# A gated Mamba block with a mixture of experts on one Trainium2 core: another table of items for the four scan batches

## What is computed

```
x  = silu(conv4(in_proj @ ctx) + conv_b)             # 512 channels x 512 steps, a causal convolution of 4 taps
dt_low, B, C = split(x_proj @ x)                     # 16 + 16 + 16 rows
dt = softplus(dt_proj @ dt_low + dt_proj_b)
for each state n of 16, each channel d of 512:
    h[n,d,t] = exp(dt[d,t] * A[d,n]) * h[n,d,t-1] + dt[d,t]*x[d,t]*B[n,t]
y[d,t] = sum over n of h[n,d,t] * C[n,t]  + D[d]*x[d,t]
x_tok += tanh(g) * y * silu(layernorm(x_tok))        # z is the layernorm of the tokens
```

## Time and profile before

| | us |
|---|---|
| median of 3 runs | 1016.52 (1015.74 to 1017.32) |
| the profiled execution's own time | 1012.7 |
| span of its trace | 1010.9 |
| scans of batches 0, 1, 2, 3 | 122.9, 109.3, 102.8, 95.5 |
| from the first scan to the end of the last | 430.5 |

### The profile page before, as it was taken

The page is one execution under the profiler, slowest core; times in us unless marked ns, Lnnn a source line. Parts: engine busy times, 40 slices in busy tenths (PEclk is TensorE's granted clock), DMA queues, the critical chain, the costliest instruction groups (busy, mean ns, idle before and its releaser), DMA issues.

```text
span 1010.9 us, 20635 instructions
## 1 busy us (share of the span) xinstructions
PE 891.2 (88%) x5397; PEld 752.7 (74%) x5397; DVE 738.8 (73%) x1112; ACT 593.1 (59%) x1006; POOL 571.0 (56%) x504
## 2 busy tenths in 40 slices
PE   6898789887988878877999999899999999974796
PEld 3465677566756767766999999899999898863795
DVE  5888989999999999999676676444554554555376
ACT  3669989797989999893332133334544444543121
POOL 5246996888968998987011057232534534531363
PEclk9799979999999999999999999999999999995699
DMA  8106111420115114113111157654657766664476
GB/s 278 44 21 229 33 42 43 154 89 31 53 38 205 42 48 135 44 49 120 42 42 42 53 174 297 213 191 168 232 182 237 238 184 237 227 199 132 139 246 225
DMA packets 65870, 136.39 MB, mean 135 GB/s; under 512 B 8833, under 2 KB 13441, under 8 KB 65666
## 3 DMA queue, kind: packets, MB, share of 16 engines
q1 hardware_dynamic: 54528, 104.68, 31.9%
q0 software_dynamic: 8960, 29.37, 8.1%
q10 hardware_dynamic: 2306, 1.33, 0.6%
HBM read 162.48 MB, written 42.07 MB: 202 GB/s over the span
## 4 chain that ended last, share of the span: by engine, by line
PE 33%; SPq 5%; POOL 5%; issue 5%; ACT 2%; DVE 2%; ACTq 1%; DMA 1%; POOLq 0%; DVEq 0%
PE psY L993 10%; PE psG L957 9%; PE psU L957 9%; POOL slot_in L641 3%; PE psT L950 2%; PE psHT L971 2%; POOL weights L666 1%; SPq L469 1%; SPq L525 1%; SPq L524 1%; ACT weights L1258 1%; SPq L526 1%; SPq L463 1%; SPq L509 1%; DMA xin<-xn_rows 1%
## 5 line engine op out<-in xcount | busy, mean ns | idle before, releaser
L597 POOL TENSOR_TENSOR prod<-hst,cbc 128x512 f32<-128x512 f32 x256 | 327.4, 1312 | 76.6 <-PE y_ps L804 39.5
L1507 DVE TENSOR_TENSOR_SCAN hst<-dA,dbu_ps 128x512 f32<-128x512 f32 x256 | 298.8, 1202 | 20.1 <-issue 10.1
L782 PE MATMUL dbu_ps<-ident,dbuT 128*128 128x128 f32 x1008 | 165.6, 288 | 45.9 <-DVE hst L1507 37.0
L782 PEld LDWEIGHTS dbu_ps<-ident,dbuT 128*128 128x128 f32 x1008 | 115.0, 145 | 107.8 <-DVE hst L1507 68.3
L1305 ACT CAST hh<-psHT 128x384 fp32r<-128x384 f32 x79 | 37.8, 478 | 252.8 <-PE psHT L971 252.8
L1179 ACT ACTIVATE dbuT<-duT,BT 128x512 f32<-128x512 f32 x252 | 160.7, 709 | 17.5 <-PE dbu_ps L782 15.6
L1169 ACT ACTIVATE dA<-dts,Aneg 128x512 f32<-128x512 f32 x256 | 166.4, 709 | 0.2
L804 PE MATMUL y_ps<-ident,prod 128*128 128x128 f32 x1024 | 159.1, 281 | 6.0 <-POOL prod L597 5.3
L957 PE MATMUL psU<-weights,xh 128*128 (+2 forms) x560 | 142.8, 337 | 0.0
L957 PE MATMUL psG<-weights,xh 128*128 (+1 forms) x560 | 137.7, 328 | 4.4 <-DVE xl L1756 3.8
L993 PE MATMUL psY<-weights,hh 128*128 (+3 forms) x420 | 134.1, 400 | 5.7 <-DVE hl L1750 3.3
(11 more groups left out here) (218 smaller groups left out, 1341.7 us busy)
## 6 DMA issues: line engine op xcount, KB each, us to landing
raw_gu<-in_L_ffn_w_gate_up_dram SPq DMA_DIRECT2D x100, 704.0 KB
raw_d<-in_L_ffn_w_down_dram SPq DMA_DIRECT2D x50, 512.0 KB
cbc<-c_rows SPq DMA_DIRECT2D x64, 256.0 KB, 3.2
slot_in<-ztile SPq DMA_DIRECT2D x3, 4096.0 KB, 13.9
gbuf<-slot_in SPq DMA_DIRECT2D x48, 256.0 KB, 3.2
slot_out<-yout POOLq DMA_DIRECT2D x48, 256.0 KB, 3.7
raw_d<-in_L_ffn_w_down_dram SPq DMA_DIRECT2D x50, 192.0 KB
xn_rows<-xin SPq DMA_DIRECT2D x16, 256.0 KB, 2.0
```

Source lines behind the costliest of these rows:

```text
L597: pool.tensor_tensor(prod[:, prod_slot(n, j), :], hst[:, slot_of(n, j), :], cbc[:, n % 2, :], ALU.mult).then_inc(prod_ready, 1)
L782: last = tr(dbu_ps[j % 2][:, t * P:(t + 1) * P], dbuT[:, n % 2, t, j * P:(j + 1) * P], ident[:])
L1507: V.tensor_tensor_scan(hst[:, slot_of(n, j), :], dA[:, slot_of(n, j), :], dbu_ps[j % 2][:], 0.0, ALU.mult, ALU.add).then_inc(scanned, 1)
```

## The change

Every entry of the table may take another item number. Besides this, (1,2) in batch 0 goes from the eight-product form to the four-tap form, (2,0) in batch 0 and (3,0) in batch 1 go the other way; the z copies of batch 2 move from DVE to ACT, those of batch 3 from ACT to DVE; `terms` goes to 0 in batch 0 and to -1 in batch 3; `z_var` moves from item 10 to 6 and `z_scale` from 16 to 10. Some banks change.

```diff
-            dict(skip=7, silu=21, x_proj=(19, 20, 21, 22), xdbl=22, bt=33, bt_copy=33, dt=(23, 27, 37, 44),
-                 softplus=(25, 31, 45, 49), rounds=(24, 31, 41, 44), log=(23, 30, 39, 44),
-                 dt_sum=(26, 36, 42, 49), du=(26, 37, 44, 51), du_turn=(30, 43, 51, 55),
-                 du_copy=(30, 43, 51, 55), du_on_act=False,
-                 conv=[(1, 0, 0, (-1, -1, -1, -1, -1, -1, -1, -1), (-1,)), (2, 0, 1, (25, 26), (26, 27, 28, 29)), (2, 1, 1, (35, 36), (40, 40, 41, 42)), (1, 1, 0, (0, 1), (5, 5, 6, 7)), (1, 2, 1, (1, 2, 3, 4, 5, 6, 7, 8), (12,)), (1, 3, 0, (11, 12), (13, 13, 14, 15))],
-                 ctx=(14, 17), ctx_copy=(15, 17), z_turn=(46, 47, 53, 57), z_copy=(51, 54, 58, 62),
-                 z_on_act=True, terms=-1),
-            dict(skip=9, silu=17, x_proj=(16, 17, 18, 19), xdbl=19, bt=34, bt_copy=34, dt=(21, 29, 38, 42),
-                 softplus=(24, 35, 42, 45), rounds=(25, 35, 39, 49), log=(25, 34, 37, 46),
-                 dt_sum=(28, 37, 41, 54), du=(31, 39, 52, 57), du_turn=(32, 47, 52, 59),
-                 du_copy=(32, 47, 52, 59), du_on_act=False,
-                 conv=[(2, 2, 1, (7, 8), (7, 7, 8, 9)), (2, 3, 0, (6, 7), (7, 7, 8, 9)), (3, 0, 1, (26, 27), (28, 28, 29, 30)), (3, 1, 1, (36, 37), (37, 37, 38, 39))],
-                 ctx=(15, 22), ctx_copy=(15, 23), post=7, z_turn=(41, 50, 57, 58), z_copy=(45, 55, 60, 62),
-                 z_on_act=True, stats=(9, 13, 24, 63), terms=-1),
-            dict(skip=5, silu=17, x_proj=(15, 16, 17, 18), xdbl=19, bt=24, bt_copy=24, dt=(23, 29, 37, 47),
-                 softplus=(25, 32, 40, 53), rounds=(24, 32, 43, 50), log=(23, 31, 42, 47),
-                 dt_sum=(26, 35, 46, 52), du=(32, 37, 50, 55), du_turn=(37, 45, 56, 58),
-                 du_copy=(37, 45, 56, 58), du_on_act=False,
-                 conv=[(3, 2, 1, (8, 9), (9, 9, 10, 11)), (3, 3, 0, (4, 5), (5, 5, 6, 7))], post=3,
-                 z_turn=(27, 30, 46, 48), z_copy=(27, 35, 47, 53), z_on_act=False, stats=(18, 25, 37, 60),
+            dict(skip=5, silu=17, x_proj=(14, 15, 16, 17), xdbl=17, bt=32, bt_copy=33, dt=(18, 23, 34, 45),
+                 softplus=(22, 27, 39, 55), rounds=(19, 25, 36, 50), log=(18, 29, 37, 48),
+                 dt_sum=(21, 33, 42, 54), du=(21, 41, 48, 55), du_turn=(35, 46, 55, 59),
+                 du_copy=(35, 46, 55, 59), du_on_act=False,
+                 conv=[(1, 0, 0, (-1, -1, -1, -1, -1, -1, -1, -1), (-1,)), (2, 0, 1, (20, 21, 22, 23, 24, 25, 26, 27), (27,)), (2, 1, 1, (36, 37), (37, 37, 38, 39)), (1, 1, 0, (2, 3), (2, 2, 3, 4)), (1, 2, 0, (6, 7), (8, 8, 9, 10)), (1, 3, 1, (3, 4), (5, 5, 6, 7))],
+                 ctx=(13, 18), ctx_copy=(13, 18), z_turn=(42, 48, 52, 58), z_copy=(46, 55, 59, 62),
+                 z_on_act=True, terms=0),
+            dict(skip=7, silu=13, x_proj=(9, 11, 13, 15), xdbl=15, bt=35, bt_copy=35, dt=(21, 33, 43, 51),
+                 softplus=(25, 36, 44, 55), rounds=(26, 34, 43, 53), log=(26, 35, 42, 51),
+                 dt_sum=(30, 38, 47, 56), du=(35, 43, 55, 58), du_turn=(36, 52, 57, 59),
+                 du_copy=(36, 52, 57, 59), du_on_act=False,
+                 conv=[(2, 2, 1, (2, 3), (3, 3, 4, 5)), (2, 3, 0, (0, 1), (1, 1, 2, 3)), (3, 0, 1, (23, 24, 25, 27, 28, 29, 31, 32), (33,)), (3, 1, 1, (39, 40), (41, 42, 43, 45))],
+                 ctx=(12, 16), ctx_copy=(12, 17), post=5, z_turn=(47, 53, 55, 58), z_copy=(50, 55, 58, 60),
+                 z_on_act=True, stats=(28, 35, 35, 50), terms=-1),
+            dict(skip=7, silu=15, x_proj=(12, 13, 14, 15), xdbl=15, bt=18, bt_copy=18, dt=(17, 26, 34, 46),
+                 softplus=(21, 31, 39, 52), rounds=(20, 29, 43, 51), log=(20, 29, 42, 49),
+                 dt_sum=(24, 32, 45, 55), du=(33, 39, 45, 57), du_turn=(36, 47, 49, 57),
+                 du_copy=(36, 47, 49, 57), du_on_act=False,
+                 conv=[(3, 2, 0, (3, 4), (4, 4, 5, 6)), (3, 3, 1, (5, 6), (5, 5, 6, 7))], post=5,
+                 z_turn=(23, 41, 45, 52), z_copy=(36, 44, 49, 58), z_on_act=True, stats=(22, 24, 29, 44),
                  terms=-1),
-            dict(skip=5, silu=11, conv=[], post=3, z_turn=(9, 20, 31, 40), z_copy=(15, 29, 35, 45), z_on_act=True,
-                 terms=0),
+            dict(skip=7, silu=10, conv=[], post=5, z_turn=(8, 17, 32, 35), z_copy=(10, 28, 32, 43), z_on_act=False,
+                 terms=-1),
...
+                if b == 0 and i == 6:
+                    z_var(0, NT, 0)
                 if b == 0 and i == 10:
-                    z_var(0, NT, 0)
-                if b == 0 and i == 16:
                     z_scale()
```

## The result

The changed kernel is slower: 1020.43 us (median of 20 runs) against 1017.06 (20 runs), ratio 1.0038, 95% interval 1.0023 to 1.0052 (one disturbed run before, of 1047.6, is left out of the ratio). Forecast was 1012.5, in a range of 1007.0 to 1018.0. The profiled execution has a span of 1019.3 us, 8.4 more than the one before. The medians differ by only 3.4.

What follows compares the result with a forecast made beforehand. DVE was taken to bound the four scan batches, 404.4 us work plus 26.1 idle. Batch terms of -3.05, -1.05, -1.3 and +1.4 gave -4.0, so 1016.5 became 1012.5 us; range 1007.0 to 1018.0.

Steps and rivals of the forecast that it cites:

- The gap ahead of the fifth scan and those around the skip: Batch 0: gap before the scan falls from 2.87 to 0.5 us (-2.4); gaps of 1.53 and 0.52 go (-2.05).
- The run of eight: Batch 0, items 20 to 27: PE needs longer than DVE for the eight-product convolution; charged +3.5 us idle.
- The waits of the softplus chains: Batch 0: chains now stand 10 or more items apart, so DVE's waits fall from 3.6 to 1.0 us (-2.6).
- Shared ports ... I take nothing: DVE rounds and du products beside POOL: 2.1 us could be won and as much lost; charged zero.
- The rival for this side: POOL holds up 24 DVE rounds and du products more; with 0.3 us each, 1019.7 us; chance 0.04.
- x_proj ... nothing in the others: Still four x_proj pieces of 0.99 us per batch; charged +0.5 us in batch 0, nothing in other batches.
- Softplus chains ... -1.7: Batch 1: DVE's late waits, about 3.2 us, fall to 1.5, a gain of 1.7.
- the rival of the late exp: ACT is late for the rounds, each item short costing 1.12 us; with six, 1019.2 us; chance 0.13.
- Skip two items behind post: Batches 1 to 3: skip always two items behind post; only batch 3 lacks another DVE piece there, +0.5 us.
- The run of eight in batch 1: Items 23 to 32: PE needs longer than DVE by 2.0 to 3.5 us, taken +2.75.
- ACT in batch 2: z copies bring ACT to 97.6 us against DVE's 96.2, no longer hidden: +1.3 us idle.
- Batch 3: DVE work +2.6 us from z copies, waits for ACT's decays -1.7, skip +0.5: together +1.4.

Runs made afterwards that it cites:

- e7: Changed kernel with POOL's products on the first 8 of 512 columns only, y mostly left out; ran once, 1000.2 us.
- e3: Changed kernel with the 4 MB of zeros of each batch written by four 1 MB transfers; ratio 1.0004 to the kernel before.
- e6: e3 with one softplus chain of batch 2 moved later and post and skip of batch 3 at 3 and 5; ratio 1.0004.
- e9: e3 plus 36 unread identity transposes on PE at items 6 and 7 of batch 1, ahead of the skip block; ratio 0.9987.
- e5: e3 with (3,0) of batch 1 back in the four-tap form, at the items of the kernel before; ratio 1.0034.
- e1: New table entry for batch 0 with z_var and z_scale, old entries for batches 1 to 3; ratio 0.9968 to the kernel before.
- e10: e9 with the old entry for batch 2 and the skip of e6 for batch 3; ratio 0.9972 to the kernel before.

## Why the prediction was wrong

**What bounds the kernel, and batch 0: right.** The gap ahead of the fifth scan and those around the skip went; only 0.37 us of waiting is left. Batch 0 gained 3.9 us, forecast 3.05. That the sum came near is partly luck, since three terms were off against each other. The run of eight cost 0.8 us of idle, not 3.5: PE needs 1.73 us per item, and DVE's `dt_sum`, `du` and rounds filled it. The waits of the softplus chains came to 2.2 (0.65 for the log, 0.73 and 0.66 for decays, 0.20), not 1.0. And DVE's work in the batch rose by 1.0.

**"Shared ports ... I take nothing": the first failed step.** The mechanism was named and the row read, but the sum took zero. It measured +4.9 us (e7 against both traces). The step also looked at the rounds alone. The rival for this side, with a chance of 0.04, priced 24 rounds and `du` products at 0.17 to 0.3 us more each; they took 0.10 more each. The splittings of batch 3, which the change does not touch, lost about as much in four operations: their mean went from 1546 to 2091 ns, and nearly all of it is the first, 3.31 us instead of 1.65, which now meets POOL at another moment.

**"x_proj ... nothing in the others": the second.** The waits at the pieces were 0.55 us in batch 1 and 0.79 elsewhere, near the forecast of 0.89. But the items of `x_proj` were also what let the 4 MB of zeros pass. POOL then waited 7.9 us for the rows of C; splitting the transfer gave back 6.1 us in the profile (e3), of which 4.1 are idle time, and about 0.3% in the timed ratios. The scan phases of e6 and e9, which have the four transfers too, took 434.6 and 434.4, that of e5 439.9. This transfer was in neither the sum nor the rivals.

**"Softplus chains ... -1.7" in batch 1: wrong for the same reason.** The late waits fell from 3.2 to 0.9, more than forecast, but at item 30 came 1.35 for PE and 1.90 for the log, and both are gone in e3. The rounds did not wait for ACT at all: no row of L1480 has idle time. So the rival of the late exp, the likeliest on the slower side, did not happen, and what waited was the step behind, `dt_sum` for the log. I had counted ACT's lead and not POOL's lag. With a lag of two to three products at 1.28 us and two subtractions of 1.28, a log three items ahead of its `dt_sum` is late even with POOL never starved: 1.77 us in batch 2 of e3. With thin products (e7) all waits for the log come to 0.6 us.

**Skip two items behind post: mis-sized.** Charged 0.5 in batch 3 and nothing in batch 1, where I counted convolution pieces that had moved ahead of `post`. In batch 3 the waits around the block went from 0.6 to 1.1, as charged, though to 2.1 in e3 and e5, where the block ran partly at half clock (0.69 granted). In batch 1 they measured 2.1 and before nothing; about 0.8 of it is the clock (e3 against e9).

**The run of eight in batch 1: near.** 2.5 us of waits at items 22 to 34, of which 0.66 stay in e5 without the run; so 1.8, forecast 2.0 to 3.5. **ACT in batch 2: small.** ACT was busy for 97.8 us as counted, and DVE waited 0.9 us for its decays, forecast 1.3. **Batch 3:** the 2.0 us of waits for decays went, as forecast; the 1.1 that the view puts down to ACT is the wait at item 8, which e6 removes by moving the skip. DVE's work rose by 4.3 instead of 2.6, by the splittings.

Open: why the medians differ by less than the profiled executions. In all ten comparisons (the changed kernel and e1 to e10 without e7) the timed difference to the kernel before is 1.6 to 6.0 us smaller than that of the scan phases. So the 430.5 of its one trace are probably short by some 4 us, an estimate from these differences, and of the 9.4 us of loss only about half would be seen on average. Why is not known. Open is also a part of batch 2: e3 is still 3.4 over the kernel before. The log makes 1.4 of it, and `du_copy`, in the same items as `du_turn`, waits 1.6 us for PE where it waited for nothing before; that these belong together is read from the trace and not tested.

## What to carry to other kernels

A piece that is slow on one engine can be the cover of a transfer on another queue. Before moving it, list what SP issues in that stretch, and how long the last thing behind it may take. When only the order of work changes, count the lag of the slowest follower (here POOL) as carefully as the lead of the engine in front. And take a price for operations that share ports from a run in which the partner is thin, rather than zero: here order alone was worth 5 us of it. A trace of each kernel was not enough to size a change of 0.4%: it showed where to look, and the timed ratios of single repairs had to say how much.

## What the runs showed of the hardware

- These operations of DVE on SBUF have a floor that is seen best without POOL's products (e7): 0.41 us for the round (up to 1.5 beside POOL), 0.87 for a splitting of 128 x 704 (up to 3.7), 0.17 for one of 128 x 16 (1.2).
- A 256 KB load of 3.1 us took 10 to 11 when issued 5 us behind a 4 MB transfer of its own queue. The same 4 MB in four pieces of 1 MB delayed no load so far that POOL waited.
- 36 transposes of the identity, which nothing reads, kept PE at 2.4 GHz across a stretch with waits behind which it was otherwise granted half, and made the block behind them 2.1 to 2.5 us shorter.
